# An attention block with its feed-forward layer on one core: the stacking matmuls contract over 64 rows instead of 128, and the last four query blocks are taken in reverse

## The reference

```python
h = layernorm(x) * (1 + ca) + sa
q, k, v = h @ Wq.T, h @ Wk.T, h @ Wv.T           # 8 heads of 16 features
scores = (q @ k.T) / 4, masked to key <= query
x = x + ga * (softmax(scores) @ v)
h = layernorm(x) * (1 + cb) + sb
p = softmax(h @ gate_W.T); cnt = number of experts over / not over 0.3
x = x + gb * (sum_e (h @ expert_W[e]) * cnt_e * p_e) @ out_W.T   # experts 0 and 1 alone count
```

## Time and profile before

| | |
|---|---|
| three runs | 256.54, 256.59, 257.93 us; median 256.59 |
| span of the profiled execution | 255.7 us (its time outside the span is not listed; the median lies 0.9 us above the span) |
| busy, share of span | PE 95%, DVE 82%, ACT 73%, POOL 31% |
| reductions of maxima (L832) | the first starts at 13.75 us, the last ends at 218.6 us |
| last product with v ends | 243.05 us |

### The profile page before, as it was taken

The page is one execution under the profiler, slowest core; times in us unless marked ns, Lnnn a source line. Parts: engine busy times, 40 slices in busy tenths (PEclk is TensorE's granted clock), DMA queues, the critical chain, the costliest instruction groups (busy, mean ns, idle before and its releaser), DMA issues.

```text
span 255.7 us, 6573 instructions
## 1 busy us (share of the span) xinstructions
PE 242.8 (95%) x2436; PEld 154.8 (61%) x2436; DVE 209.6 (82%) x524; ACT 187.5 (73%) x407; POOL 78.9 (31%) x126
## 2 busy tenths in 40 slices
PE   8999999999999989999999999899999999999923
PEld 3686666656565445467666675565676667666512
DVE  4389999999998989999999989899999999223034
ACT  2556767587986849589848897777997589999910
POOL 7864562357920441045100331003310002310010
PEclk9999999999999999999999999999999999999965
DMA  6300000000000001000001000000000000000000
GB/s 173 115 4 0 5 5 0 3 3 3 0 4 3 4 0 42 3 0 3 2 15 32 3 1 3 25 1 3 3 3 3 22 4 3 0 4 24 0 0 21
DMA packets 5742, 3.42 MB, mean 13 GB/s; under 512 B 488, under 2 KB 5552, under 8 KB 5712
## 3 DMA queue, kind: packets, MB, share of 16 engines
q1 hardware_dynamic: 5136, 2.56, 3.4%
q10 hardware_dynamic: 576, 0.46, 0.6%
HBM read 1.84 MB, written 1.05 MB: 11 GB/s over the span
## 4 chain that ended last, share of the span: by engine, by line
PE 90%; DVE 4%; ACT 3%; issue 2%; POOLq 0%; POOL 0%; DVEq 0%; ACTq 0%
PE ctx_ps L1075 25%; PE ps L1037 19%; PE ps L1051 18%; PE ps L1094 7%; PE ps L1058 4%; PE ps L1133 3%; PE ps L1165 3%; PE ctx_ps L1083 2%; PE ps L1160 2%; DVE part_max L832 2%; PE ps L1154 2%; PE ps L1127 2%; PE ps L1147 2%; PE ps L1140 2%; ACT probs L733 1%
## 5 line engine op out<-in xcount | busy, mean ns | idle before, releaser
L832 DVE TENSOR_REDUCE part_max<-ps 128x1 f32<-128x512 f32 (+3 forms) x288 | 170.3, 652 | 6.5 <-PE ps L1051 4.5
L733 ACT ACTIVATE probs<-ps 128x512 f32<-128x512 f32 x208 | 103.3, 612 | 17.2 <-PE ps L1037 16.4
L1037 PE MATMUL ps<-q_stack,k_stack 50*128 50x256 f32 (+3 forms) x512 | 86.9, 324 | 0.1
L1051 PE MATMUL ps<-k_stack,q_stack 48*128 48x512 f32 (+3 forms) x320 | 85.9, 418 | 0.0
L1075 PE MATMUL ctx_ps<-probs,v_aug 128*32 128x256 f32 (+3 forms) x1024 | 72.8, 399 | 0.1
L1037 PEld LDWEIGHTS ps<-q_stack,k_stack 50*128 50x128 f32 x512 | 58.1, 186 | 21.4 <-DVE part_max L832 6.0
L1051 PEld LDWEIGHTS ps<-k_stack,q_stack 48*128 48x128 f32 x320 | 45.3, 185 | 19.7 <-DVE part_max L832 6.3
L730 ACT ACTIVATE probs<-ps 128x512 f32<-128x512 f32 (+3 forms) x96 | 41.0, 501 | 10.9 <-PE ps L1037 10.1
L703 POOL TENSOR_SCALAR_AFFINE_SELECT probs<-probs 128x512 f32<-128x512 f32 x32 | 20.2, 637 | 90.5 <-ACT probs L733 72.5
L1075 PEld LDWEIGHTS ctx_ps<-probs,v_aug 128*32 128x32 f32 x1024 | 26.1, 109 | 23.0 <-issue 4.8
L1058 PE MATMUL ps<-mask_half,ident_half 64*128 64x128 bf16 x256 | 27.0, 222 | 0.0
(11 more groups left out here) (94 smaller groups left out, 177.0 us busy)
## 6 DMA issues: line engine op xcount, KB each, us to landing
x_sb<-in_L_attn_hidden_states SPq DMA_DIRECT2D x3, 256.0 KB, 5.2
out_x<-result SPq DMA_DIRECT2D x2, 256.0 KB, 2.3
out_x<-result SPq DMA_DIRECT2D x4, 128.0 KB, 1.8
x_sb<-in_L_attn_hidden_states SPq DMA_DIRECT2D x2, 128.0 KB, 2.8
wmod<-in_L_wmod ACTq DMA_DIRECT2D x1, 256.0 KB, 5.5
q_stack<-max_row SPq DMA_DIRECT2D x16, 4.0 KB
wmod<-in_L_wmod ACTq DMA_DIRECT2D x1, 128.0 KB, 2.8
expert_w<-in_L_ffn_expert_W SPq DMA_DIRECT2D x1, 128.0 KB, 5.1
```

What stands on the lines that cost most here:

```text
L733: drained(act.activation(probs[:, :, prob_columns(b)].rearrange("p (n e) q -> p e n q", e=2)[:, e], bank.rearrange("p (n q) -> p n q", n=2 ...
L832: dve.tensor_reduce(part_max[:, n % 2, i, heads[0]:heads[-1] + 1:2, c], banks[:, 0, 0:len(heads) * width].rearrange("p (e k) -> p e k", k= ...
L1037: last = pe.matmul(out_at, k_stack[at:at + rows, p, j * P:(j + 1) * P], q_stack[at:at + rows, p, tile * P + q0:(tile + tiles) * P], start= ...
L1051: last = pe.matmul(banks[:, 0, m * width:(m + 1) * width], q_stack[at:at + ROWS, p, tile * P:(tile + 1) * P], k_stack[at:at + ROWS, p, c * ...
```

## The change

Two things are edited, and with them the order table and some assumed costs.

1. A spread's two matmuls contract over the 64 rows that hold its pair of heads (rows 0 to 63 for pairs 0 and 1, rows 64 to 127 for pairs 2 and 3) instead of all 128. The rows left out meet zeros of the matrix, so what is computed stays. The number of matmuls, their columns and ACT's copies are the same.
2. The four blocks of two tiles are taken as tiles 14-15, 12-13, 10-11, 8-9. Block 14-15 needs the keys of all 16 tiles, block 8-9 those of ten.

The stream A holds the spreads of pairs 0 and 1; those of pairs 2 and 3 go to a new stream B. `ORDER` is another table over the same 988 steps.

```diff
-BLOCKS = [(0, 4), (4, 4), (8, 2), (10, 2), (12, 2), (14, 2)]
+BLOCKS = [(0, 4), (4, 4), (14, 2), (12, 2), (10, 2), (8, 2)]
...
+def low_spreads(g):
+    return spreads(g)[:4]
+def high_spreads(g):
+    return spreads(g)[4:]
...
-    if s[0] in ("scores", "maxima"):
+    if s[0] in ("scores", "maxima", "spread"):
         return "rows"
...
-        A=[("project", 1, 1), ("project", 1, 0)] + spreads(1)[:4] + spreads(0)[4:] + spreads(1)[4:]
-        + [s for g in range(SPLIT_GROUPS, NG) for s in prepare(g)[1:-1]],
+        A=[("project", 1, 1), ("project", 1, 0)] + low_spreads(1)
+        + [s for g in range(SPLIT_GROUPS, NG) for s in prepare(g)[1:4] + low_spreads(g)],
+        B=[s for g in range(NG) for s in high_spreads(g)],
...
 ORDER = (
-    "TVATAMMMMTTAAAAAAMMMMMMAVVAAAAAAMMMXXXMMMAVTTXAVMMMMMMAMMSVXAAXASMSMTSMMASSXMMSSMMTSMSXSMMMMMMSPAAMS"
+    "BTTTTTAAVVBAAVBMMBMBBMAMABTMAMMMMMMAXXAVMXMTMBTMMXVMAMBMMAMMBABMAMVSMSBMMMMXSAMMMSXSSASXMMSMMXASSTMM"
...
+                    at = TILE * (p // 2)
                     for m in range(2):
-                        last = pe.matmul(bank[:, 0:width], spread[:, qk, m, p].rearrange("p e r d -> p (e r d)"),
-                                         piece[m][:, g % 2, qk, 0:width], start=m == 0, stop=m == 1)
+                        last = pe.matmul(bank[:, 0:width],
+                                         spread[at:at + TILE, qk, m, p].rearrange("p e r d -> p (e r d)"),
+                                         piece[m][at:at + TILE, g % 2, qk, 0:width], start=m == 0, stop=m == 1)
```

More of the change, by code:

```diff
@@ L230, in estimate @@
         if score_slots(n) == HALF:
-            return [(s[2] % 2, w / 2.4 + 22)], [("act", w * 0.833 + 51)] + mask, 175
-        return [(s[2], w / 2.4 + 15)] * 2, [("act", 2 * w * 0.833 + 51)] + mask, 175
+            return [(s[2] % 2, w / 2.4 + 32)], [("act", w * 0.833 + 51)] + mask, 175
+        return [(s[2], w / 2.4 + 20)] * 2, [("act", 2 * w * 0.833 + 51)] + mask, 175
     if kind == "maxima":
         w = maxima_width(s[1], s[2], s[4])
-        t = w / 2.4 + 18 + (134 if s[4] == key_chunks(s[1]) - 1 else 0)
+        t = w / 2.4 + 18 + (165 if s[4] == key_chunks(s[1]) - 1 else 0)
         return [(s[3][0] % 2, t * len(s[3]))], [("vec", len(s[3]) * w * 1.042 + 63)], 145
@@ L238, in estimate @@
         return [(None, sum(score_width(*batches[b]) * 4 / 2.4 + 8 for b in item_passes()[s[1]]))], [], PROBS_V_PASSES
+    if kind == "spread":
+        w = GROUPS[s[1]][1] * P
+        return [(s[2] // 2, 2 * (w / 2.4 + 15))], [("act", w * 0.833 + 38 + 106 * s[3])], 200
     if kind == "warm":
@@ L246, in estimate @@
         share = (GROUPS if s[1] == "stats" else BLOCKS)[s[2]][1] / TG
-    elif kind in ("stats2", "normalize2", "norm2_t", "ffn"):
+    elif kind in ("stats2", "normalize2", "norm2_t", "ffn", "logits"):
         share = BLOCKS[s[1]][1] / TG
@@ L337, in needs_of @@
         for qk in range(2):
-            needs[projection(g, qk)] = [("norm_t", g)] + ([("spread", g - 2, PAIRS - 1, 0)] if g >= 2 else [])
+            needs[projection(g, qk)] = [("norm_t", g)] + ([("spread", g - 2, p, qk) for p in range(PAIRS)] if g >= 2 else [])
             for p in range(PAIRS):
@@ L360 @@
 ORDER = (
-    "TVATAMMMMTTAAAAAAMMMMMMAVVAAAAAAMMMXXXMMMAVTTXAVMMMMMMAMMSVXAAXASMSMTSMMASSXMMSSMMTSMSXSMMMMMMSPAAMS"
[L362 to L370, removed]
+    "BTTTTTAAVVBAAVBMMBMBBMAMABTMAMMMMMMAXXAVMXMTMBTMMXVMAMBMMAMMBABMAMVSMSBMMMMXSAMMMSXSSASXMMSMMXASSTMM"
+    "SSPSTMSSMBAMMMPTSSMMSSMSPMSMSTBAMMSAMMPMEMSAXMPAESSMMMXMAXMMSMMSSXAMMBMAMSPSMMMSMSVMMESABMPPEMSSMMSE"
+    "SAEBMMSVASEXBXMMSSPSESEXBMSMMSPSESSMMSMMXVSMMSSMVSMMSSMMEMMMBSSESMMSSMPPMSSESMMEPMEMMESSSPMSSMSMSEMS"
+    "MEXPSSMEMSSPSSMXMMMSEESMSSXSPPSMMMSSPSMMMSSXEMMMSMSPPMMSSESMPSMSMMSPMSMSMSPMESMSMSSEESSMMSESPPSSMMSS"
+    "SPEXPMSMSMSPXPMSMEESMXSPMSMSSMPPMMMSMSXEMSMSPMSMSPMMMSSSEMSMSEEMSPPMSMESMSSEXSEPMEMEMSMSPPMMEMESSSPP"
+    "PXPMMMSXMSPPMSSMMSEXMSMSMSPPMSMSMSPMSMSPMSMSMSPPMSMMSMMESPPPMSMSSMPEMSXMSMSPPEMSMSPXEMSESSSEMMEXPPSS"
+    "ESSMMMPPMSMSMMPEXMSMSSSEMSMSMMPPEESSESMMSPPEMSMSESSEXXPXEMSSMMSPEEXEMSMSPPMSMMMSPPMSMSMSPPMSSSSMPPMS"
+    "MSMMSSXPPMXSMSMSEPPMSMSMSPPMESSMSMMSSEEESSSEEMSEMSPXPPPMSSMMSSPPXESSSSSMMPEMSMESMSPMSMESXEXEXMSPSESS"
+    "ESSPPPEEEXEPPSSSSSMMPPPMMMESSSSPPSSMMSSMPMSMSMSPPPPMESSSEMSMSSSPEEPEMSMSMSXXSEXSSSPPPEXESSSSSEEPPSES"
+    "SPSESSSESSPEPEEEESSSSSPPPSSSSSSPPPPPPPEEEEEEEEEEEEEEEEEEE")
 def plan():
@@ L649, in _ @@
                     pool.wait_ge(act_drained, act_slot[step] + 1)
-                    pool.wait_ge(act_filled, act_slot[("spread", g - 2, PAIRS - 1, 0)] + 1)
+                    pool.wait_ge(act_filled, max(act_slot[("spread", g - 2, p, qk)] for p in range(PAIRS)) + 1)
                     pool.tensor_copy(piece[0][:, g % 2, qk, :], wide[:, qk, :]).then_inc(pool_pieces, 1)
```

2 lines of the change are left out of this document (1 added, 1 removed).

## The result

The changed kernel takes **246.69 us** (median of 4 runs, 246.37 to 247.55) against 257.26 (256.54 to 259.25) for the kernel before in the same comparison: ratio 0.960, 95% interval 0.955 to 0.965. The forecast was 252.1 with a range from 247.5, so it has the right sign and less than half of the gain. The profiled execution has a span of 245.8 us against 255.7.

What follows compares the result with a forecast made beforehand. DVE was taken as pacemaker from 14 to 184 us. From the 255.7 us span, -2.5 (64-row spreads) and -2.0 (reversed blocks) gave 251.2, plus 0.9 to the median: 252.1 us, range 247.5 to 256.8.

Steps and rivals of the forecast that it cites:

- What bounds the kernel: DVE paces 14 to 184 us, busy 160.7 of 170 us; later stretches read separately, the last 12.8 us one chain.
- term one: Spreads over 64 rows free 7.8 us of PE; gain -2.5 us, capped by DVE's 5.0 us idle in 14 to 97 us.
- the preparation pulled forward: Eight last-group spreads, a normalized transpose and two ACT copies move from after 97 us to before it; costed at nothing.
- 6 or 7: Sign for the size of term one: DVE's idle time, first to 240th reduction, falls to 6 or 7 us.
- PE starved DVE all along: Rival: 7 us less on PE lets DVE run end to end, 14 to 184 us; 246.6 us, chance 0.14.
- What PE saved: Half of the spread matmuls' 15.6 us, 7.8 us, freed on PE; some 6.9 us after six more mode changes.
- The reversed blocks: Last 48 maxima 40.3 us, stretch after the last maximum 16.7: 57.0 against 59, -2.0 us (ends -5.5 and -0.3).
- at or after 220: Sign for the reversed blocks: the last reduction ends at or after 220 us, about 17 us before the last product.
- The last chain: Short steps of the last block at the end: same twelve steps, 12.7 us, change 0, at most +0.8.
- The rule against it: ACT's copies out of PSUM, 22.2 us over 40 spreads, already pace runs of spreads; by it term one is nil.
- The slower rival: Spreads' pieces come late from POOL, so PE, maxima and DVE wait at six places; 259.7 us, chance 0.12.

Runs made afterwards that it cites:

- e4: Kernel before, with its 224 wide reductions reading 480 of 512 columns: 257.2 us, ratio 1.000.
- e1: Kernel before, with each spread issuing one of its two matmuls: 256.1 us, ratio 0.994.
- e3: Changed kernel, in its order and with its banks, with spreads over 128 rows again: 262.8 us, ratio 1.024.
- e7: Order searched anew, 128-row spreads as in the kernel before, but two-tile blocks reversed: 254.2 us, ratio 0.986.
- e6: Order searched anew, with 128-row spreads and ascending blocks as in the kernel before: 254.4 us, ratio 0.988.
- e9: Both edits of the changed kernel (64-row spreads, reversed blocks), order searched anew from another start: 249.5 us, ratio 0.970.
- e10: e8 with the gates' step moved 16 steps later: one execution 252.1 us, nine others 255.0 to 262.5 (median 256.2).
- e2: Kernel before, in its order and with its banks, with 64-row spreads: 265.0 us, ratio 1.018.
- e12: e3 with one 128-row matmul per spread instead of two: median 261.0 us; the one run at the usual clock 256.3.
- e8: Order searched anew, with 64-row spreads and ascending blocks: 260.4 us, ratio 1.011.

## Why the prediction was wrong

**What bounds the kernel: wrong.** From 14 to 184 us "DVE is the pacemaker", it said, and "the other 7.8 - 2.5 is hidden under DVE". The rows had a second reading: PE was busy 62.30 of 62.40 and 105.36 of 107.70 us, DVE idle 9.3 us. e4 takes 7.5 us of columns from DVE and nothing happens. e1 takes 7.8 us from PE and 1.4 to 2.1 come back. So neither engine is hidden by the other, and the order decides how much of PE's time can be won. My picture is that the two hand seven banks back and forth in a list that both keep to; no run tests the banks by themselves.

**The step that failed** is term one, -2.5 us, with its cap, "cannot exceed those 5.0", and with the stretch from 97 to 184 us put at nothing. It measured -9.2 (the 240th reduction, 183.9 to 174.7 us). I capped the gain by DVE's idle time in 14 to 97 us, because the spreads are there, and wrote: "From 97 to 184 us DVE's 4.3 us of idle time stay: only 16 spread matmuls leave". About there, from the 96th to the 240th reduction, 8.1 us were won. Those 16 with their projections were a preparation of four tiles in the middle of a stretch that PE also filled. They could leave because half-array spreads made room for them earlier: +14 spread matmuls before the 96th reduction and no time lost, where the same order with whole-array spreads (e3) takes 74.6 us for what takes 60.1. I costed "the preparation pulled forward" at nothing as a burden on ACT and POOL (right) and did not see it as a relief of PE 50 us later. DVE's idle time went to 2.4 us, not to "6 or 7". Of the 10.4 us from first to 240th reduction (170.1 to 159.7), 6.9 is idle time and 3.5 is DVE's work done elsewhere, 1.8 of it before the first reduction (6.07 to 7.89). The rival "PE starved DVE all along", at 246.6 us and with a chance of 0.14, comes nearest. That its time was met is partly luck: its split (-6 and -4) was not (-9.2 and -0.7), and by e1 less work on PE does not feed DVE in the old order, where DVE's idle time from the 96th to the 240th reduction stayed at 6.5 us (6.8 before).

**What PE saved: right in number, in part by luck.** 7.8 us was forecast as freed, 6.9 after the mode changes, and PE's busy time is 7.8 us less. But that is the sum of two larger numbers: in the new order the row halves take 16.3 us off it (251.3 in e3, 235.0), and with whole-array spreads that order has 8.5 us more than the old one. Between orders searched for each, the row halves are worth 4.0 to 4.5 us (e7 and e6 against e9). What I did not price is that the 208 mode changes of the new order would be 250 with whole-array spreads.

**The reversed blocks: right, the size smaller.** Forecast 40.3 + 16.7 = 57.0 us to the last product; measured from the 240th reduction to the start of the last product 58.0 (before 58.8), and to the end -0.7 against -2.0, inside its ends -5.5 and -0.3. ACT is 88% busy in the last 48 maxima (37.30 of 42.4), not over 90. The last reduction ended at 217.8, not "at or after 220": everything before it was earlier. In the searched orders reversal was worth 0.2 us with whole-array spreads; the 2.6 us with half-array ones rest on one execution of e10.

**The last chain: right**, 13.0 us from the start of the last product to the end, before and after.

**The rule against it: does not decide here.** ACT's copies of the spreads take as long as ever (page of the changed kernel, idle time before them last):

```profile
L754 ACT ACTIVATE k_stack<-ps,shift_ones 128x512 fp32r<-128x512 f32 (+1 forms) x20 | 11.7, 616 | 0.7 <-PE ps L1107 0.6
L756 ACT CAST q_stack<-ps 128x512 fp32r<-128x512 f32 (+1 forms) x20 | 9.8, 505 | 2.1 <-PE ps L1107 1.8
```

But a spread is no longer in a row of spreads: beside it runs work whose banks DVE reads. By the prediction's rule term one would be nil, and 9.2 us were measured up to the 240th reduction; e2, where the spreads stay in rows, is nearest to the rule's case and gained nothing, though its clock keeps that from being clean. The rule leans on the Trainium skill ("TensorEngine Tiling (Array Packing)", section "PSUM Bottleneck"), which says that tiling speeds up TensorE but not the reading out of PSUM. The Trainium skill ("TensorEngine Tiling (Array Packing)", section "Key Properties") also says that a change of tiling mode drains TensorE. e12's 0.23 us for each change agrees with that, but lost overlap is in the number.

**The slower rival: did not happen.** No group of spreads waited for POOL in the first 90 us; PE idles 0.34 us in the 60.1 from the first to the 96th reduction.

**Open:** how the 9.9 us divide between 64 rows, reversal and search can't be told to better than the two or three microseconds by which orders of the same steps differ (249.5 and 246.7). What paced the old order, in which e1 and e4 give back so little, stays open too. What makes the clock fall in e2 and in most runs of e10 and e12 was not settled either: no hole comes first in e2's profile, and e12 has no 64-row spread.

## What to carry to other kernels

An engine that is 98% busy is not covered by another that is 95% busy: count both as bounds, and test each by taking work from it, since the busy share alone told neither (e1, e4). Cut the two runs at equal progress, and look at the work that is left behind the cut, before a gain is put down to a stretch. A matmul that uses half the array is cheap only where its neighbours in the list use the other half, so the edit and the order are one change, and testing either alone (e2: 1.8% slower, part of it the clock; e3: 2.4% slower) does not tell what the pair does (4% faster). Look at what a cheaper step lets the order pull forward: the gain shows where that work has gone away.

## What was not expected of the hardware

- A 128x2 instruction of DVE took 2.90 us in e8 beside POOL's work and ended with POOL's memset (28.02 and 27.99 us); in e10, at a later place, it took 0.169. The Trainium skill ("Perfetto Trace Analysis", section "Optimizing Scalar/DVE Operations") says that GpSimd and DVE share a read port and that DVE can hold it as an exclusive lock; here the wait looks the other way round, DVE behind POOL, as far as one instance shows it.
- A hole of 1.83 us in PE's stream, in a stretch of 64-row spreads (PE busy 3.17 of the 5 us from 26 to 31), was followed by 13.7 us at 1.2 GHz. e10, that order with one step moved, ran at 2.4 GHz up to its last 10 us in one execution of ten. The changed kernel's profile has no such stretch before 238 us.
